# First convolution of a four-layer block: nine taps in five groups of 128 rows, with a second set of copies

## The chip, the cores and the metric

The kernel runs on one core of a Trainium2 chip. The metric is the device time of one execution in microseconds; several executions are run and their median is given. A core has five engines that run their own instruction streams and meet only at semaphores: TensorE (PE in the profile; PEld are its weight loads), VectorE (DVE), ScalarE (ACT), GpSimd (POOL) and SyncE (SP, which here only issues DMAs). Sixteen DMA engines move data.

## The reference

Input x is 32 images of 64 channels, 28 x 28 pixels, in float32. Four layers follow one another, each of the form `x = x + layer(group_norm(x))`. The change touches only the first, a convolution whose 3 x 3 weights are mixed per image from four candidates:

```
pooled = mean(x, axis=(2, 3));  h = relu(pooled @ fc1_w.T)
prob = softmax((h @ fc2_w.T + fc2_b).reshape(B, 4, 64) / 4, axis=1)
agg_w = einsum('bko,koihw->boihw', prob, weight)     # 64 x 64 x 3 x 3 per image
out = conv(x, agg_w), 3 x 3, stride 1, padding 1, one set of weights per image
```

Layer 1 is a quantised convolution, layer 2 a two-dimensional cosine transform, layer 3 self-attention over the 784 pixels with four heads.

## The kernel before, in words

All 32 images stay on the chip as 16 pairs: an image has 64 channels, so a pair fills the 128 partitions (image 0 of the pair in partitions 0 to 63, image 1 in 64 to 127). Layers run one after another over all pairs. Every engine has its own program for a layer (`l0` for the first), written with four pairs unrolled, a loop over the middle ones, and two unrolled at the end; `pair_steps` and `looped` do that. The order on each engine is the order of the text.

The first convolution, pair p, goes through these steps:

- **mix** (DVE, lines 1265 to 1277): four operations of 128 x 576 on the candidates `w0` give the pair's weights `agg[p % 2]`, output channels in partitions, taps and input channels along the row.
- **pad** (DVE, line 1285): each image is normalised into its own padded tile of 30 x 30, `pads[p % 2][im]`, image 0 in partitions 0 to 63 and image 1 in 64 to 127. After the second of them `s_pad` rises.
- **twin** (SP, lines 416 and 417): two DMAs fill the other 64 partitions of the two tiles with the same image shifted by one pixel. So 128 partitions hold two horizontally neighbouring taps, and one matmul over 128 rows does both.
- **transposes** (PE, lines 832 to 840): `agg` is turned so that input channels lie in partitions, in six transposes: three of two taps (128 rows out) and three of the single third tap of an image row (64 rows out). ACT (lines 652 and 653) copies them to `pair_w` and `last_w`.
- **convolution** (PE, line 861): for each half c of the image (14 image rows, 392 columns) twelve matmuls accumulate into one bank: three of 128 rows (the first two taps of each row of the 3 x 3 window) and three of 64 rows (the third tap), each for both images of the pair. The two images' matmuls use different halves of the array's columns. The transposes of pair p + 1 stand between the two halves of pair p.
- **add, statistics** (DVE, lines 1300 and 1170 to 1173): each half is added to x when it is done, and after the second half the statistics for the next layer are taken; then comes pad of pair p + 2.

Before the first matmul of a pair PE waits for the copied weights (line 845) and for the twins (line 846):

```
pe.wait_ge(s_convw, lin(lambda q: q + 1, p, i, 2))
pe.wait_ge(s_twin[p % 2], lin(lambda q: 32 * (q // 2 + 1), p, i, 2))
```

Tiles are doubled by p % 2, and pad of pair p + 2 waits for the end of pair p's convolution, since it writes the tile that pair p reads. All float32 matmuls appear as two records each in the profile (two passes).

Of the kernel before, what the change touches and what calls it, by code (L numbers as in the profile page):

```python
# [14 lines left out]
B, C, H, W = 32, 64, 28, 28  # L15
T = H * W
NP = B // 2
HC = H // 2
CH = HC * W
BANK = 512  # L20
HID, KEXP = 16, 4
NG, GC = 4, 16
HP, WP = H + 2, W + 2
# [16 lines left out]
ACT = mybir.ActivationFunctionType  # L40
# [14 lines left out]
    _at += _width  # L55
PARAMS = _at
W0_COLS = KEXP * C * 9
W1_ROWS = GC * 3 * 2
W1_COLS = NG * 3 * 128

# [5 lines left out]
def build(nc, x_in, params, w0_in, w1_in, out):  # L66
    ctx = ExitStack()
    with ctx:
# [6 lines left out]
        x = sb("x", [128, NP, T])  # L75
        par = sb("par", [128, PARAMS])

        def P(name, rows=128):
            return par[0:rows, AT[name][0]:AT[name][1]]
# [24 lines left out]
        def part(shape, dt=F32):  # L104
            n = int(np.prod(shape[1:])) * mybir.dt.size(dt) // 4
            a = arena[0:shape[0], cut[0]:cut[0] + n]
            cut[0] += n
            assert cut[0] <= ARENA, cut[0]
            if dt is not F32:
                a = a.bitcast(dt)  # L110
            names = " ".join("abcde"[:len(shape) - 1])
            if len(shape) > 2:
                a = a.rearrange(f"p ({names}) -> p {names}", **dict(zip("abcde", shape[1:])))
            return a


        w0 = part([128, KEXP, 9 * C])
        agg = [part([128, 9, C]) for _ in range(2)]
        pair_w = [part([128, 3, 128]) for _ in range(2)]
        last_w = [part([C, 3, 128]) for _ in range(2)]  # L120


        PAD = HP * WP + 4
        pads = [[part([128, PAD]) for _ in range(2)] for _ in range(2)]
        pooled = part([128, NP])
        hid = part([2 * HID, NP])
        logit = part([128, NP, KEXP])
# [52 lines left out]
        ps = ctx.enter_context(nc.psum_tensor("ps", [128, 8, BANK], F32))  # L180
# [16 lines left out]
        def lin(f, s0, i, per):  # L197

            return f(s0) if i is None else i * (f(s0 + per) - f(s0)) + f(s0)
# [17 lines left out]
        s_convw = sem("s_convw")  # L217
        s_pad = sem("s_pad")
        s_twin = [sem(f"s_twin{n}") for n in range(2)]
# [177 lines left out]
        def _(sp):  # L397
# [14 lines left out]
            def twin_step(p, i):  # L412

                first, second = pads[p % 2]
                wait_apart(sp, s_pad, lin(lambda q: q + 1, p, i, 2))
                sp.dma_start(first[C:2 * C, 0:HP * WP - 1], first[0:C, 1:HP * WP]).then_inc(s_twin[p % 2], 16)
                sp.dma_start(second[0:C, 1:HP * WP + 1], second[C:2 * C, 0:HP * WP]).then_inc(s_twin[p % 2], 16)

            pair_steps(twin_step, sp)

# [216 lines left out]
        def _(act):  # L637
# [9 lines left out]
            def l0(p, i):  # L647

                act.wait_ge(s_aggt, lin(lambda q: q + 1, p, i, 2))
                if p >= 2:  # L650
                    act.wait_ge(s_conv, lin(lambda q: 2 * (q - 1), p, i, 2))
                nc.scalar.activation(pair_w[p % 2].rearrange("p y n -> p (y n)"), ps[:, 0, 0:3 * 128], ACT.Copy)  # L652
                nc.scalar.activation(last_w[p % 2].rearrange("p y n -> p (y n)"), ps[0:C, 1, 0:3 * 128],
                                     ACT.Copy).then_inc(s_convw, 1)

            pair_steps(l0, act)

# [144 lines left out]
            n = at_ring(B - 1, NU - 1) + 1  # L802
# [4 lines left out]
        def _(pe):  # L807
# [16 lines left out]
            for k in range(KEXP):  # L824
                last = nc.tensor.matmul(ps[:, 5, k * NP:(k + 1) * NP],
                                        P("fc2", 2 * HID)[:, k * 128:(k + 1) * 128],
                                        hid[:, :], start=True, stop=True)
            last.then_inc(s_l0t, 1)

            def l0_transpose(p, i):  # L830

                pe.wait_ge(s_agg, lin(lambda q: q + 1, p, i, 2))
                if p >= 1:
                    pe.wait_ge(s_convw, lin(lambda q: q, p, i, 2))
                for y in range(3):
                    n = slice(y * 128, (y + 1) * 128)
                    nc.tensor.transpose(ps[:, 0, n],
                                        agg[p % 2][:, 3 * y:3 * y + 2, :].rearrange("p t i -> p (t i)"), P("ident"))
                    last = nc.tensor.transpose(ps[0:C, 1, n], agg[p % 2][:, 3 * y + 2, :], P("ident"))  # L839
                last.then_inc(s_aggt, 1)  # L840

            def l0(p, i):
                if p == 0:
                    l0_transpose(0, None)
                pe.wait_ge(s_convw, lin(lambda q: q + 1, p, i, 2))
                pe.wait_ge(s_twin[p % 2], lin(lambda q: 32 * (q // 2 + 1), p, i, 2))
                for c in range(2):
                    bank = 3 + 2 * (p % 2) + c
                    if p >= 2:
                        pe.wait_ge(s_added, lin(lambda q: 2 * (q - 2) + c + 1, p, i, 2))  # L850


                    for single in range(2):
                        for y in range(3):
                            for im in range(2):
                                rows = slice(0, C if single else 128)
                                w = (last_w if single else pair_w)[p % 2][:, y, im * C:(im + 1) * C]
                                at = (y + c * HC) * WP + 2 * single + im
                                rhs = pads[p % 2][im][rows, at:at + HC * WP].rearrange(
                                    "p (y x) -> p y x", x=WP)[:, :, 0:W]  # L860
                                last = nc.tensor.matmul(ps[im * C:(im + 1) * C, bank, 0:CH], w, rhs,  # L861
                                                        start=(y == 0 and not single), stop=(y == 2 and single == 1))
                    last.then_inc(s_conv, 1)
                    if c == 0 and p + 1 < NP:
                        l0_transpose(p + 1, i)
# [278 lines left out]
            n = at_ring(B - 1, NU - 1) + 1  # L1144
# [7 lines left out]
        def _(dve):  # L1152
# [54 lines left out]
                chain[0], chain[2] = start + links * rounds, None  # L1207


            for pair in pads:  # L1210
                for b in pair:
                    last = v.memset(b[:, :], 0.0)
# [49 lines left out]
            def mix(p, i):  # L1262

                pr = at_pair(p, i)
                a = agg[p % 2].rearrange("p t i -> p (t i)")

                def weight(k):
                    return prob[:, bass.ds(pr, 1), k]

                if p >= 2:  # L1270
                    dve.wait_ge(s_aggt, lin(lambda q: q - 1, p, i, 2))
                link(v.tensor_scalar(a, w0[:, 0, :], weight(0), None, ALU.mult))
                for k in range(1, KEXP):
                    last = v.scalar_tensor_tensor(a, w0[:, k, :], weight(k), a, ALU.mult, ALU.add)
                    if k < KEXP - 1:
                        link(last)
                last.then_inc(s_agg, 1)
# [233 lines left out]
def pack(a):  # L1511
# [16 lines left out]
    n = W  # L1528
# [28 lines left out]
    put("head_rows", np.kron(np.eye(NH, dtype=f), np.ones((1, 2 * DK), f)), slice(0, NH))  # L1557


    w0 = a["L0_conv_weight"].transpose(1, 0, 3, 4, 2).reshape(C, W0_COLS)  # L1560
    w0 = np.ascontiguousarray(np.tile(w0, (2, 1)))

    w1 = a["L1_conv_weight"].reshape(C, NG, GC, 3, 3).transpose(2, 4, 1, 3, 0)
# [18 lines left out]
```

## Time and profile before

| | us |
|---|---|
| median of 3 runs | 1832.68 |
| lowest, highest | 1827.34, 1839.15 |
| the profiled execution's own time | 1829.92 |
| its span | 1828.1 |
| mean granted clock of PE | 0.949 |

| engine | busy us | share of the span |
|---|---|---|
| PE | 1663.0 | 91% |
| DVE | 1285.1 | 70% |
| ACT | 1022.2 | 56% |
| POOL | 434.1 | 24% |

The first convolution lies between 62.3 and 212.9 us of the span. Times in the rows are counted from the span's start. A row of the timeline gives start, duration, engine, line, operation, output and input tile and number of instructions, merged where they follow one another; in brackets stands the idle time before and what ended it. SPq is the queue of DMA issues: such a row is the issuing, not the transfer. "PEclk" is the granted clock as a share of full speed: 1.00 is 2.4 GHz, 0.50 is 1.2 GHz.

### The profile page before, as it was taken

How to read it: one execution, taken by the hardware profiler on the slowest of the kernel's cores; microseconds unless marked ns; L12 is line 12 of the kernel's file. 1: busy time of each engine (PE TensorE's matmuls, PEld its weight loads, DVE VectorE, ACT ScalarE, POOL GpSimd, SP SyncE). 2: the span in 40 equal slices, each digit the busy share in tenths (PEclk: the TensorE clock that was granted, in tenths of full speed). 3: DMA queues.
4: the chain of work that ended last, by engine and by line, in shares of the span. 5: the costliest groups of instructions: out<-in, count | busy, mean ns of one | idle time of the engine just before them, and what ended most of it. 6: DMA issues, size and time to landing. Idle time of an engine off the chain costs nothing.

```text
span 1828.1 us, 35089 instructions
## 1 busy us (share of the span) xinstructions
PE 1663.0 (91%) x10910; PEld 751.8 (41%) x10910; DVE 1285.1 (70%) x2603; ACT 1022.2 (56%) x1401; POOL 434.1 (24%) x333
## 2 busy tenths in 40 slices
PE   0799689997884999999999999999999999999997
PEld 0333245554873244444434434434443443444332
DVE  5677467887784887777767767666776776767762
ACT  0100166674331176777767667666676776767676
POOL 0400011112102212423413223232341423323111
PEclk9999899999897599999999989989999999999999
DMA  8111166663002332332233322332322332224300
GB/s 197 41 51 45 40 108 100 109 102 54 0 0 33 50 43 33 48 58 43 35 48 50 49 43 33 47 51 46 48 33 43 53 53 43 33 47 54 47 11 19
DMA packets 70267, 93.31 MB, mean 51 GB/s; under 512 B 22648, under 2 KB 63224, under 8 KB 69968
## 3 DMA queue, kind: packets, MB, share of 16 engines
q1 hardware_dynamic: 67728, 89.59, 29.9%
q0 software_dynamic: 2368, 1.57, 1.0%
q8 instruction: 92, 1.51, 0.3%
q14 instruction: 79, 0.65, 0.1%
HBM read 9.00 MB, written 6.42 MB: 8 GB/s over the span
## 4 chain that ended last, share of the span: by engine, by line
PE 81%; DVE 6%; ACT 4%; DMA 3%; SPq 3%; issue 3%; DVEq 0%; POOL 0%; ACTq 0%; POOLq 0%
PE ps L1051 20%; PE ps L1041 18%; PE ps L986 16%; PE ps L861 8%; PE ps L885 5%; PE ps L900 3%; PE ps L1032 3%; PE ps L1007 2%; ACT arena L679 2%; DMA x<-x_in 2%; PE ps L947 2%; SPq L433 2%; PE ps L1024 1%; DVE arena L1430 1%; PE ps L1015 1%
## 5 line engine op out<-in xcount | busy, mean ns | idle before, releaser
L1430 DVE TENSOR_REDUCE arena<-ps 128x1 f32<-128x392 f32 x1600 | 827.0, 559 | 329.5 <-PE ps L986 316.1
L792 ACT ACTIVATE arena<-ps 112x784 f32<-112x784 f32 x896 | 703.4, 822 | 270.4 <-PE ps L1041 265.8
L986 PE MATMUL ps<-arena 112*128 112x392 bf16 x1536 | 491.1, 348 | 8.7 <-DMA arena<-arena 8.2
L1041 PE MATMUL ps<-arena 114*112 114x392 bf16 x1792 | 457.1, 342 | 19.9 <-issue 14.8
L1051 PE MATMUL ps<-arena 112*32 112x392 f32 x3584 | 401.2, 520 | 0.4 <-ACT arena L792 0.4
L986 PEld LDWEIGHTS ps<-arena 112*128 112x128 bf16 x1536 | 151.2, 99 | 377.4 <-DVE arena L1430 307.5
L1041 PEld LDWEIGHTS ps<-arena 114*112 114x112 bf16 x1792 | 230.2, 136 | 140.7 <-issue 50.8
L885 PE MATMUL ps<-arena 96*128 96x392 f16 x768 | 142.2, 336 | 22.0 <-DMA arena<-arena 16.5
L679 ACT ACTIVATE arena<-ps,magic,arena 128x784 f32<-128x784 f32 x128 | 128.2, 1004 | 37.2 <-PE ps L885 37.0
L861 PE MATMUL ps<-arena 128*64 128x392 f32 (+1 forms) x768 | 139.5, 505 | 3.9 <-DMA arena<-arena 3.9
L1051 PEld LDWEIGHTS ps<-arena 112*32 112x32 f32 x3584 | 71.3, 109 | 147.7 <-issue 146.0
L885 PEld LDWEIGHTS ps<-arena 96*128 96x128 f16 x768 | 67.5, 98 | 95.3 <-ACT arena L679 29.4
L529 POOL TENSOR_TENSOR arena<-arena 128x784 f16<-128x784 f32 x16 | 26.0, 1626 | 324.9 <-ACT arena L668 324.9
L1337 DVE TENSOR_SCALAR arena<-arena 128x784 bf16<-128x784 f32 x128 | 73.1, 571 | 32.3 <-ACT arena L679 21.6
L600 POOL TENSOR_TENSOR arena<-arena 128x784 f32<-128x784 f32 x31 | 57.4, 1852 | 122.3 <-ACT arena L749 122.3
L861 PEld LDWEIGHTS ps<-arena 128*64 128x64 f32 (+1 forms) x768 | 49.6, 135 | 86.4 <-issue 84.2
L652 ACT ACTIVATE arena<-ps 128x384 f32<-128x384 f32 x16 | 7.9, 492 | 134.3 <-PE ps L839 134.3
L595 POOL DMA_DIRECT2D arena<-arena x31 | 21.3, 687 | 251.8 <-DVE arena L1445 234.6
L694 ACT ACTIVATE arena<-ps 112x512 f32<-112x512 f32 x64 | 31.0, 542 | 67.9 <-PE ps L944 67.8
L569 POOL TENSOR_TENSOR x<-x,arena 128x784 f32 (+1 forms) x16 | 29.6, 1853 | 161.4 <-DVE arena L1423 161.4
L900 PE MATMUL ps<-arena 128*64 128x392 bf16 x768 | 66.5, 329 | 0.0
L628 POOL TENSOR_TENSOR x<-x,arena 128x784 f32 (+1 forms) x15 | 27.9, 1863 | 160.0 <-ACT arena L743 160.0
(139 smaller groups left out, 1381.9 us busy)
## 6 DMA issues: line engine op xcount, KB each, us to landing
arena<-arena SPq DMA_DIRECT2D x504, 73.5 KB, 2.7
arena<-arena SPq DMA_DIRECT2D x256, 84.2 KB, 2.8
x<-x_in SPq DMA_DIRECT2D x8, 784.0 KB, 21.2
out<-x SPq DMA_DIRECT2D x16, 392.0 KB, 2.4
arena<-arena SPq DMA_DIRECT2D x252, 24.5 KB, 2.3
arena<-arena SPq DMA_DIRECT2D x256, 1.5 KB
arena<-arena SPq DMA_DIRECT2D x16, 225.0 KB, 3.4
arena<-arena SPq DMA_DIRECT2D x16, 224.8 KB, 2.9
```

The source lines that it names most:

```text
L600: nc.gpsimd.tensor_tensor(a, a, den[:, :], ALU.mult).then_inc(s_head, 1)
L679: nc.scalar.activation(halves(rounded[u % 4]), two(2 * (u % 2)), ACT.Identity, bias=magic[:, 0:1], scale=ratio[:, u % NG:u % NG + 1]).then ...
L792: nc.scalar.activation(probs[w % 2][:, 2 * pair:2 * pair + 2, :], two(2 * place, rows=slice(0, TT)), ACT.Exp).then_inc(s_taken, 1)
L861: last = nc.tensor.matmul(ps[im * C:(im + 1) * C, bank, 0:CH], w, rhs, start=(y == 0 and not single), stop=(y == 2 and single == 1))
L885: last = nc.tensor.matmul(ps[:, 2 * (u % 2) + c, 0:CH], w1[:, g, y, :], rhs, start=(y == 0), stop=(y == 2))
L900: last = nc.tensor.matmul(ps[im * C:(im + 1) * C, bank + c, 0:CH], sdiag[:, k, g, :], quant[2 * (p % 2) + im][:, g, c * CH:(c + 1) * CH], ...
L986: last = nc.tensor.matmul(ps[:, bank, 0:CH], q[0:ROWS_L, h, it * 128:(it + 1) * 128], k[0:ROWS_L, h, c * CH:(c + 1) * CH], start=True, sto ...
L1032: last = nc.tensor.matmul(ps[:, 2 * place + c, 0:CH], P("head_rows", NH), den_row[:, c * CH:(c + 1) * CH], start=True, stop=True)
L1041: last = nc.tensor.matmul(ps[0:TT, 2 * place + j, 0:CH], ks[s % 4][0:ROWS_ALL, h, jt * TT:(jt + 1) * TT], qs[s % 4][0:ROWS_ALL, h, c * CH: ...
L1051: last = nc.tensor.matmul(ps[32 * h:32 * h + 32, BANK_ACC, 0:CH], vs[s % 4][:, jt, h, :], probs[w % 2][:, h, :], start=(jt == 0), stop=(jt ...
L1337: link(v.tensor_scalar(capped[:, :], rounded[u % 4][:, :], MAGIC, QP, ALU.subtract, ALU.min))
L1430: nc.vector.tensor_reduce(mx[img % 2][:, c, v:v + 1], scores, AX.X, ALU.max).then_inc(s_mf, 1)
```

## The change

The nine taps are stored in another order, `TAPS`: the first two of each row of the window, then the three third taps, and a tenth place in `agg` that is set to zero once. Five groups of two taps (`UNITS`) replace three groups of two and three of one. Groups 0 to 2 are as before. Group 3 holds the third taps of the window's rows 0 and 1; it reads new tiles, `rows_pads`, whose partitions 0 to 63 hold the image and 64 to 127 the image shifted up by one row (30 elements). Group 4 holds the third tap of row 2 beside the zero weights and reads `pads`. Four DMAs more per pair fill the two new tiles, two for each image; PE now waits for six DMAs of a pair (96) in place of two (32). There are five transposes of 128 x 128 in place of six, and the two ACT copies take 512 and 128 columns of all partitions.

```diff
+TAPS = [(y, x) for y in range(3) for x in range(2)] + [(0, 2), (1, 2), (2, 2)]
+UNITS = 5
-        agg = [part([128, 9, C]) for _ in range(2)]
-        pair_w = [part([128, 3, 128]) for _ in range(2)]
-        last_w = [part([C, 3, 128]) for _ in range(2)]
+        agg = [part([128, 2 * UNITS, C]) for _ in range(2)]
+        pair_w = [part([128, UNITS, 128]) for _ in range(2)]
+        rows_pads = [[part([128, HP * WP]) for _ in range(2)] for _ in range(2)]
...
                 sp.dma_start(second[0:C, 1:HP * WP + 1], second[C:2 * C, 0:HP * WP]).then_inc(s_twin[p % 2], 16)
+                for to, data in zip(rows_pads[p % 2], (first[0:C], second[C:2 * C])):
+                    sp.dma_start(to[0:C, :], data[:, 0:HP * WP]).then_inc(s_twin[p % 2], 16)
+                    sp.dma_start(to[C:2 * C, 0:(HP - 1) * WP], data[:, WP:HP * WP]).then_inc(s_twin[p % 2], 16)
...
-                for y in range(3):
-                    n = slice(y * 128, (y + 1) * 128)
-                    nc.tensor.transpose(ps[:, 0, n],
-                                        agg[p % 2][:, 3 * y:3 * y + 2, :].rearrange("p t i -> p (t i)"), P("ident"))
-                    last = nc.tensor.transpose(ps[0:C, 1, n], agg[p % 2][:, 3 * y + 2, :], P("ident"))
+                for n in range(UNITS):
+                    last = nc.tensor.transpose(ps[:, n // 4, (n % 4) * 128:(n % 4 + 1) * 128],
+                                               agg[p % 2][:, 2 * n:2 * n + 2, :].rearrange("p t i -> p (t i)"),
+                                               P("ident"))
...
-                pe.wait_ge(s_twin[p % 2], lin(lambda q: 32 * (q // 2 + 1), p, i, 2))
+                pe.wait_ge(s_twin[p % 2], lin(lambda q: 96 * (q // 2 + 1), p, i, 2))
...
-                    for single in range(2):
-                        for y in range(3):
-                            for im in range(2):
-                                rows = slice(0, C if single else 128)
-                                w = (last_w if single else pair_w)[p % 2][:, y, im * C:(im + 1) * C]
-                                at = (y + c * HC) * WP + 2 * single + im
-                                rhs = pads[p % 2][im][rows, at:at + HC * WP].rearrange(
-                                    "p (y x) -> p y x", x=WP)[:, :, 0:W]
-                                last = nc.tensor.matmul(ps[im * C:(im + 1) * C, bank, 0:CH], w, rhs,
-                                                        start=(y == 0 and not single), stop=(y == 2 and single == 1))
+                    for n in range(UNITS):
+                        y, x_ = TAPS[2 * n]
+                        for im in range(2):
+                            by_rows = n == 3
+                            src = (rows_pads if by_rows else pads)[p % 2][im]
+                            at = (y + c * HC) * WP + x_ + (0 if by_rows else im)
+                            rhs = src[:, at:at + HC * WP].rearrange("p (y x) -> p y x", x=WP)[:, :, 0:W]
+                            last = nc.tensor.matmul(ps[im * C:(im + 1) * C, bank, 0:CH],
+                                                    pair_w[p % 2][:, n, im * C:(im + 1) * C], rhs,
+                                                    start=(n == 0), stop=(n == UNITS - 1))
...
+            for a in agg:
+                v.memset(a[:, 9, :], 0.0)
...
-    w0 = a["L0_conv_weight"].transpose(1, 0, 3, 4, 2).reshape(C, W0_COLS)
+    w0 = a["L0_conv_weight"].transpose(1, 0, 3, 4, 2)
+    w0 = np.stack([w0[:, :, y, x] for y, x in TAPS], 2).reshape(C, W0_COLS)
```

On SP, the copies of pairs 0 and 1 in the kernel before, each pair behind its own wait for `s_pad`:

```order
L416 DMA arena<-arena 64x899
L417 DMA arena<-arena 64x900
L416 DMA arena<-arena 64x899
L417 DMA arena<-arena 64x900
```

The same place in the changed kernel, pair 0 alone (then the same six for pair 1):

```order
L420 DMA arena<-arena 64x899
L421 DMA arena<-arena 64x900
L423 DMA arena<-arena 64x900
L424 DMA arena<-arena 64x870
L423 DMA arena<-arena 64x900
L424 DMA arena<-arena 64x870
```

The old two copies go first; the four new ones stand behind them in the same queue, and PE's wait is for all six.

On PE, the transposes of pair 0 and the first half of its convolution, before:

```order
L837 MATMUL ps<-par,arena 128x128
L839 MATMUL ps<-par,arena 64x128
L837 MATMUL ps<-par,arena 128x128
L839 MATMUL ps<-par,arena 64x128
L837 MATMUL ps<-par,arena 128x128
L839 MATMUL ps<-par,arena 64x128
L861 MATMUL ps<-arena 64x392 x12
```

and now, with the transposes of pair 1 and what follows them:

```order
L842 MATMUL ps<-par,arena 128x128 x5
L865 MATMUL ps<-arena 64x392 x10
L842 MATMUL ps<-par,arena 128x128 x5
L865 MATMUL ps<-arena 64x392 x20
```

Ten matmuls stand in place of twelve in each half, and nothing else has moved on PE.

## Rows read from the trace of the kernel before

**Rows 1.** The page: the chain that ended last, share of the span by line.

```profile
PE ps L1051 20%; PE ps L1041 18%; PE ps L986 16%; PE ps L861 8%; PE ps L885 5%; PE ps L900 3%; PE ps L1032 3%; PE ps L1007 2%; ACT arena L679 2%; DMA x<-x_in 2%; PE ps L947 2%; SPq L433 2%; PE ps L1024 1%; DVE arena L1430 1%; PE ps L1015 1%
```

**Rows 2.** The chain in order of time, first convolution (start us, us, what).

```profile
58.28 0.55 SPq L416
58.87 3.37 DMA arena<-arena
...
62.37 6.54 PE ps L861 x24
...
78.22 0.26 PE ps L837
...
79.03 8.51 PE ps L861 x48
...
212.96 0.57 DVE x L1300
```

**Rows 3.** Timeline of PEld, one pair: the weight loads stand where passes begin.

```profile
73.90 0.20 PEld L861 LDWEIGHTS ps<-arena 128*64 128x64 f32 x4 [0.61 <-issue]
...
76.03 0.20 PEld L861 LDWEIGHTS ps<-arena 64*64 64x64 f32 x4 [0.61 <-issue]
...
78.15 0.14 PEld L837 LDWEIGHTS ps<-par,arena 128*128 128x128 f32 x1 [0.61 <-issue]
...
78.96 0.20 PEld L861 LDWEIGHTS ps<-arena 128*64 128x64 f32 x4 [0.20 <-issue]
...
83.22 0.20 PEld L861 LDWEIGHTS ps<-arena 128*64 128x64 f32 x4 [0.61 <-issue]
```

**Rows 4.** Timeline of DVE after the last matmul of pair 0.

```profile
74.02 0.56 DVE L1300 TENSOR_TENSOR x<-x,ps 128x392 f32<-128x392 f32 x1 [1.50 <-PE ps L861]
...
76.13 1.39 DVE L1285 TENSOR_SCALAR arena<-x,gmean,grstd 64x784 f32<-64x784 f32 x2
78.27 0.56 DVE L1300 TENSOR_TENSOR x<-x,ps 128x392 f32<-128x392 f32 x1 [0.75 <-PE ps L861]
...
79.30 2.53 DVE L1274 SCALAR_TENSOR_TENSOR arena<-arena 128x576 f32<-128x576 f32 x3
```

**Rows 5.** Timeline of SP: the issue of pair 2's two copies.

```profile
77.55 0.46 SPq L416 DMA_DIRECT2D arena<-arena  x1
78.06 0.60 SPq L417 DMA_DIRECT2D arena<-arena  x1
```

**Rows 6.** Line 417, the second copy: time from issue to landing.

```profile
DMA to landing us min/median/max: 3.3/3.4/4.0
```

**Rows 7.** Windows (window, us, busy of PE, PEld, DVE, ACT, POOL, PEclk, DMA share, GB/s).

```profile
78.67:79.82 1.15, 1.15 (x10) 0.57 (x10) 1.11 (x3) 0.75 (x2) 0.00 (x0) 1.00 0.99 203
79.82:80.67 0.85, 0.85 (x9) 0.29 (x4) 0.81 (x2) 0.11 (x1) 0.00 (x0) 1.00 0.73 267
```

**Rows 8.** Timeline of PEld at the first pair's start.

```profile
63.71 0.26 PEld L861 LDWEIGHTS ps<-arena 128*64 128x64 f32 x2 [0.39 <-issue]
64.36 0.26 PEld L861 LDWEIGHTS ps<-arena 128*64 128x64 f32 x2 [0.39 <-issue]
...
67.43 0.14 PEld L861 LDWEIGHTS ps<-arena 64*64 64x64 f32 x2 [0.19 <-issue]
67.76 0.14 PEld L861 LDWEIGHTS ps<-arena 64*64 64x64 f32 x2 [0.19 <-issue]
```

**Rows 9.** Windows around two idle stretches of PE in later layers.

```profile
240.65:243.44 2.79, 0.00 (x1) 0.01 (x1) 2.51 (x5) 1.04 (x2) 0.00 (x0) 1.00 0.81 132
243.44:247.88 4.44, 4.44 (x17) 2.17 (x18) 1.41 (x4) 2.87 (x3) 1.63 (x1) 0.62 0.81 132
...
577.27:581.17 3.90, 0.00 (x1) 0.01 (x1) 3.74 (x6) 1.10 (x4) 0.35 (x1) 1.00 0.00 0
581.17:582.40 1.23, 1.23 (x4) 0.81 (x5) 0.00 (x0) 0.00 (x0) 1.22 (x3) 1.00 0.38 51
582.40:585.59 3.19, 3.19 (x6) 1.07 (x4) 0.00 (x0) 0.91 (x1) 3.19 (x8) 0.50 0.93 114
```

More of the change, by code:

```diff
@@ L651, in l0 @@
                     act.wait_ge(s_conv, lin(lambda q: 2 * (q - 1), p, i, 2))
-                nc.scalar.activation(pair_w[p % 2].rearrange("p y n -> p (y n)"), ps[:, 0, 0:3 * 128], ACT.Copy)
-                nc.scalar.activation(last_w[p % 2].rearrange("p y n -> p (y n)"), ps[0:C, 1, 0:3 * 128],
-                                     ACT.Copy).then_inc(s_convw, 1)
+                nc.scalar.activation(pair_w[p % 2][:, 0:4, :].rearrange("p y n -> p (y n)"), ps[:, 0, 0:BANK], ACT.Copy)
+                nc.scalar.activation(pair_w[p % 2][:, 4, :], ps[:, 1, 0:128], ACT.Copy).then_inc(s_convw, 1)
             pair_steps(l0, act)
@@ L1264, in mix @@
                 pr = at_pair(p, i)
-                a = agg[p % 2].rearrange("p t i -> p (t i)")
+                a = agg[p % 2][:, 0:9, :].rearrange("p t i -> p (t i)")
                 def weight(k):
```

## The prediction

> **What bounds the kernel now.** I read the page's chain first: the first convolution is 8% of it by its matmul line [rows 1], so the change can only reach that stage. The chain in order of time shows the stage's shape [rows 2]: one wait for the first pair's copies, and from 62.37 us to 212.96 nothing but matmuls and transposes, one round of 8.51 us plus transposes per pair. PE is the bound. The weight loads give the round exactly [rows 3]: pair 1 starts at 73.90 and pair 2 at 83.22, which is 9.32 us. Sixteen pairs of it make the stage.
>
> What stands next in line is not seen in the chain, and the change works on it: the time from the end of one pair's matmuls to the arrival of the copies that the pair after next needs. The rows of DVE, SP and DMA give it. Pair 0 ends at 73.90; DVE adds the second half at 74.02, takes statistics and writes the padded tiles of pair 2 until 77.52 (76.13 + 1.39) [rows 4]; SP issues the two copies at 77.55 and 78.06 [rows 5]; data moves from 78.67 to 80.67 [rows 7]; the second copy lands 3.4 us after its issue [rows 6], at 81.46. Pair 2 starts at 83.22. **The slack is 1.76 us**, and every pair has it.
>
> **PE's part of the change.** Half a pair is six passes at 128 rows (73.90 to 76.03) and six at 64 rows (76.03 to 78.15), 2.13 us each [rows 3]. Between neighbouring passes lie 0.33 us (67.43 to 67.76 [rows 8]), six of them 1.96, so each block has 0.17 us more, where the row count of the weights changes. The transposes take 78.15 to 78.96, 0.81 us. A pair is 4 x 2.13 + 0.81 = 9.33. After the change a half has ten passes, all of 128 rows: 3.27 us. The change of shape remains only before the transposes (0.17), and a transpose less at 0.11 us each leaves 0.70. A pair is 2 x 3.27 + 0.17 + 0.70 = **7.4 us of PE**, 1.9 less. Were PE still the bound, the stage would lose 15 x 1.9, about 29 us, 1.6% of the kernel.
>
> DVE could follow: after the second half it works 3.50 us (74.02 to 77.52) and after the first one 3.56 (78.27 to 81.83) [rows 4], 7.1 in all, within 7.4. The larger ACT copy sits after the transposes with 3.3 us of matmuls to hide it. The two memsets of 64 columns on DVE lie in the wait for x at the start. All of these I cost at nothing; without PE's cover DVE would set 7.1.
>
> **The copies.** Six take the place of two, all of the same size within 4%, in one queue; PE waits for the last. The two now take 1.15 and 0.85 us of data time, and in that time the DMA engines are 0.99 and 0.73 busy at 203 and 267 GB/s [rows 7]. So they are limited by moving bytes, not by issue: SP issues one in 0.5 to 0.65 us and stays ahead. Of the four new ones, two go to partitions 0 to 63 and two to 64 to 127, as one and one do now. Two more such sets cost 2 x 2.0 = 4.0 us end to end, or 2 x (0.99 x 1.15 + 0.73 x 0.85) = 3.5 if the engines never pause between them. I take **3.7**. The landing moves from 81.46 to 85.16, that is from 7.56 to 11.26 us after the pair's end; with the step to the first matmul (landing at 62.24, matmul at 62.37 [rows 2]) 11.4.
>
> The slack is gone: pair 1 begins as pair 0 ends and needs 7.4, so PE then stands idle for 11.4 - 7.4 = **4.0 us**, works off pair 2 and, its copies having come meanwhile, pair 3, and idles again. The loop is over two pairs: 11.4 + 7.4 = 18.8, and 0.05 to 0.1 for the drain, against 2 x 9.32 = 18.64 now. Seven such loops (ends of pairs 0 to 14) give +1.5 us. The first pair starts 3.7 later and ends its own work 1.9 earlier, +1.8; the last pair saves 1.8 behind the last loop. Sum without the clock: **+1.5 us**. The whole gain of PE is eaten by the later landing.
>
> **The clock.** Now PE never rests in this stage. At its start it ran at the lower of its levels: passes of a pair of images 0.65 us apart (63.71 to 64.36) and, once warm, 0.33 (67.43 to 67.76) [rows 8]; until the change at 66.98 that cost about 2.3 us (half of 62.37 to 66.98). Two idle stretches of other layers show what a rest of such length does [rows 9]: PE idle for 2.79 us, and in the 4.44 behind it the granted clock is 0.62 (most of it at 1.2 GHz); idle for 3.90 us, then 1.23 us at 1.00 and the next 3.19 at 0.50. So each gap of 4.0 should cost half of 3.4 us at least, 1.7, and up to the 2.3 of the start. I take 2.0, seven times: **+14 us**. It enters the loop fully, since the slowed pair's end starts the next copies. The Trainium skill (TensorE: Matmul & The Clock Gate, "HAM oscillation — how this bites in real kernels") describes this for a loop that waits on a DMA in each round: it restarts at the lower clock every round. By that rule all seven gaps pay; the two stretches agree.
>
> **Sum.** 1.5 + 14, about +15 us on the profiled execution's 1829.92 us: 1845. The median of the runs stands 2.8 above that execution, so 1847 for the median. The other layers keep their instructions; only addresses move.
>
> **The rivals.**
> (a) *As forecast*, copies bound the loop and the clock falls in each gap. With 3.5 to 4.0 for the copies and 1.7 to 2.3 for the clock: (-1.4 to +2.1) + (12 to 16) + 1.5, +12 to +20. For it: the DMA engines' shares and both idle stretches. Chance 0.60.
> (b) *The clock holds.* The other layers' matmuls have other shapes, and two stretches are few. +1.5: 1834. Chance 0.09.
> (c) *Faster: the four new copies move at the rate of the second copy's best, so the gap shrinks.* At 0.85 and less each, since its engines are only 0.73 busy (0.62 of busy time): 4 x 0.62 = 2.5 in place of 3.7, seven loops of -1.2, -8; gap 2.8, where a fall is not certain: 0 to +12. Between 1826 and 1838. It would be a gain above 1% from a loop of 16.0 us on (18.64 less 18.3 / 7), a landing less than 1 us later than now; PE alone would be the bound only if the copies landed no later than now, and the time 1804. Against it: 900 KB would have to move in 1 us, four times the rate of the row. Chance 0.11, of which 0.04 above 1%. The Trainium skill (DMA: Bandwidth & Descriptors, "Anatomy of one DMA — SWDGE (gpsimd) path") fits a transfer as 2.0 us plus bytes over 436 GB/s; by it the four new copies would add 2.1 us, not 3.7, and the time would be about that of this rival. The trace does not bear it out: 203 and 267 GB/s.
> (d) *Slower: all four new copies move like the first, not like the second.* The first differs from the second in its target (partitions 64 to 127) and its source address (off by one element); which counts no row tells. At 1.15 each the landing is 4.6 later, at more queueing 5.5: seven loops of +0.9 to +1.8 on top, gap 4.9 to 5.8 with the same fall or a longer one. +22 to +32: 1854 to 1864. It decides from a landing 4.2 us later. Chance 0.20.
>
> **How the numbers follow.** What this kernel's measurement can tell from no change is about 1%, 18 us. Slower by more: (d) and the upper fifth of (a), 0.20 + 0.13 = 0.33. Faster by more: 0.04. Within: 0.63. The range takes in (a) and (b), the slower half of (c) and nearly all of (d), with some 3 us for the spread of a median: 1829 to 1863. (a) alone spans 1845 to 1852.
>
> **What the new profile would show.** PEld's timeline: a pair of 7.4 us and no shape change inside a half. SP: six issues per pair in some 3.7 us. Windows: DMA share near 0.9 for 5.5 to 6 us per pair. PE: an idle stretch of about 4 us ended by the copies before every other pair (2, 4, ..., 14), and none before the odd ones. PEclk: 0.50 for 3 to 5 us behind each. Stage end near 228 us in place of 212.96. The forecast is wrong if copies of SBUF data overlap better than the two of today show, if gaps come before every pair (another loop than mine), or if later layers shift.

## The result, and the profile after

| | before | after |
|---|---|---|
| median us (runs) | 1833.28 (4) | 1858.37 (4) |
| lowest to highest | 1827.34 to 1839.15 | 1849.85 to 1861.05 |
| profiled execution, its span | 1829.92, 1828.1 | 1861.05, 1859.2 |
| mean granted clock | 0.949 | 0.933 |
| first convolution, first to last matmul | 62.37 to 212.92 | 67.00 to 237.58 |

The ratio is 1.0129, with a 95% interval of 1.0082 to 1.0176. The change makes the kernel **slower by 25 us**. The first convolution alone ends 24.7 us later (237.58 against 212.92), which is about the whole difference of the medians (25.1); the profiled execution of after is the slowest of its four, with 5 us more in the attention layer.

PE's part did what it was meant to. This is PE's timeline of the changed kernel: two rows on the form of a pair, then the rows before which PE was idle (in brackets: for how long and what ended it).

```profile
73.85 6.81 PE L865 MATMUL ps<-arena 128*64 128x392 f32 x40
...
81.29 3.51 PE L865 MATMUL ps<-arena 128*64 128x392 f32 x20
88.97 5.21 PE L865 MATMUL ps<-arena 128*64 128x392 f32 x20 [4.17 <-issue]
...
110.06 5.18 PE L865 MATMUL ps<-arena 128*64 128x392 f32 x20 [4.30 <-DMA arena<-arena]
...
132.09 6.11 PE L865 MATMUL ps<-arena 128*64 128x392 f32 x20 [5.27 <-DMA arena<-arena]
...
154.81 5.00 PE L865 MATMUL ps<-arena 128*64 128x392 f32 x20 [5.02 <-DMA arena<-arena]
...
176.42 6.13 PE L865 MATMUL ps<-arena 128*64 128x392 f32 x20 [5.04 <-DMA arena<-arena]
...
199.17 5.01 PE L865 MATMUL ps<-arena 128*64 128x392 f32 x20 [5.04 <-DMA arena<-arena]
...
220.66 6.19 PE L865 MATMUL ps<-arena 128*64 128x392 f32 x20 [4.91 <-issue]
```

The second halves of pairs 0 and 1 start at 73.85 and 81.29: a pair takes 7.44 us in place of 9.32 [rows 3]. But PE is idle for 4.2 to 5.3 us before pairs 2, 4, ..., 14, where before it was never idle ([rows 2]: 8.51 us of matmuls, transposes, 8.51 us). Each first half behind a gap takes 5.0 to 6.2 us; the same ten matmuls at full clock take 3.5. Windows over the stage, before and then after (window, us, busy of PE, PEld, DVE, ACT, POOL, PEclk, DMA share, GB/s), and over two of the slow halves:

```profile
62.37:212.92 150.55, 150.55 (x858) 58.64 (x858) 99.06 (x177) 14.18 (x31) 3.71 (x4) 1.00 0.18 46
```

```profile
67.00:237.58 170.58, 136.83 (x715) 58.12 (x715) 97.91 (x175) 12.79 (x31) 0.00 (x0) 0.90 0.52 119
88.97:94.17 5.20, 5.20 (x21) 2.29 (x22) 0.00 (x0) 0.00 (x0) 0.00 (x0) 0.67 0.93 219
132.09:138.20 6.11, 6.11 (x21) 2.21 (x22) 0.00 (x0) 0.00 (x0) 0.00 (x0) 0.57 0.89 206
```

PE's busy time fell only from 150.55 to 136.83 us although a sixth of the matmuls went, since 0.10 of the clock is missing: at half clock that is 34 us of the 170.58 (the start of the stage, slow before and after, is not recorded in PEclk). The seven slow halves (38.8 us together, against 7 x 3.52) cost **14.2 us**. The idle time costs 33.8 us (170.58 less 136.83) and the later start 4.6; PE's shorter pairs take 28 us off.

The chain through one loop, pair 4's second half to pair 6's first (start, us, what):

```profile
115.94 3.47 PE ps L865 x20
...
119.89 0.57 DVE x L1307
...
124.00 0.47 SPq L420
...
127.14 4.83 DMA arena<-arena
...
132.09 6.11 PE ps L865 x20
```

Where the chain before was PE alone, it now runs PE, DVE, SP, DMA, PE. From the second add at 119.89 to the next matmul are 12.20 us: DVE 4.11 until the issue at 124.00, and 8.09 from issue to matmul, where before 4.04 lay between (77.55 to 81.46 and the 0.13 of the step) [rows 5, 6]. So four copies more make the landing **4.05 us** later. Windows over the copies of pair 2, whose first is issued at 80.94, and the time to landing of line 424, the last of each tile:

```profile
83.00:84.00 1.00, 1.00 (x10) 0.44 (x8) 0.96 (x2) 0.00 (x0) 0.00 (x0) 1.00 0.96 295
...
86.00:87.00 1.00, 0.00 (x0) 0.00 (x0) 0.90 (x5) 0.00 (x0) 0.00 (x0) 1.00 1.04 229
87.00:88.10 1.10, 0.00 (x0) 0.00 (x0) 1.08 (x2) 0.00 (x0) 0.00 (x0) 1.00 0.73 161
```

```profile
DMA to landing us min/median/max: 4.3/4.8/6.0
```

The DMA engines are full until about 87 us, against shares of 0.99 and 0.73 with two copies [rows 7]. The new copies' first packets start 0.96 to 1.00 us apart in the trace: about 1.0 us each, whichever half of the partitions they go to and whether their source is shifted or not. The old two keep their form in the longer queue: the third copy starts 0.63 us behind the second.

### The profile page after: what moved, and what is told of

Its sections match the earlier page's. It is cut to its first block, busy times and chain, and to the rows that moved or that the text cites. A ratio compares the mean times of both kernels' runs of the same rounds, so it can differ in the third digit from the quotient of the medians.

```text
span 1859.2 us, 34867 instructions
## 1 busy us (share of the span) xinstructions
PE 1657.9 (89%) x10766; PEld 754.1 (41%) x10766; DVE 1285.3 (69%) x2605; ACT 1021.8 (55%) x1401; POOL 434.1 (23%) x333
## 4 chain that ended last, share of the span: by engine, by line
PE 77%; DVE 7%; DMA 5%; SPq 4%; issue 4%; ACT 3%; DVEq 0%; POOL 0%; ACTq 0%; POOLq 0%
PE ps L1056 19%; PE ps L1046 17%; PE ps L991 16%; PE ps L865 6%; PE ps L890 4%; DMA arena<-arena 3%; PE ps L905 3%; PE ps L1037 3%; PE ps L1012 2%; SPq L440 2%; DMA x<-x_in 2%; ACT arena L685 2%; PE ps L952 2%; PE ps L1029 1%; DVE arena L1437 1%
## 5 line engine op out<-in xcount | busy, mean ns | idle before, releaser
L865 PE MATMUL ps<-arena 128*64 128x392 f32 x640 | 127.4, 555 | 42.1 <-DMA arena<-arena 33.0
L659 ACT ACTIVATE arena<-ps 128x512 f32<-128x512 f32 x16 | 9.6, 599 | 162.7 <-PE ps L842 162.7
L1344 DVE TENSOR_SCALAR arena<-arena 128x784 bf16<-128x784 f32 x128 | 73.1, 571 | 32.3 <-ACT arena L685 21.5
L865 PEld LDWEIGHTS ps<-arena 128*64 128x64 f32 x640 | 50.2, 153 | 111.3 <-issue 110.9
```

What stands on the lines that cost most here:

```text
L1344: link(v.tensor_scalar(capped[:, :], rounded[u % 4][:, :], MAGIC, QP, ALU.subtract, ALU.min))
```

## The experiments

The theory after the result: the loop of two pairs is set by the path from a pair's end over DVE, SP and the six copies to the pair after next, and the clock falls in the gaps that this opens. Its rivals: the new form of the matmuls is slow itself; the slow halves come from PE reading beside the DMAs; one DMA queue, not the engines, is the limit. Each window row that begins at the stage's start covers the first convolution from its first to its last matmul; the stage before took 150.55 us and after 170.58. Ratios are to the kernel before, run beside each experiment.

**Copies alone** (`e1_copies_only`, on the kernel before):

```diff
+        rows_pads = [[part([128, HP * WP]) for _ in range(2)] for _ in range(2)]
...
+                for to, data in zip(rows_pads[p % 2], (first[0:C], second[C:2 * C])):
+                    sp.dma_start(to[0:C, :], data[:, 0:HP * WP]).then_inc(s_twin[p % 2], 16)
+                    sp.dma_start(to[C:2 * C, 0:(HP - 1) * WP], data[:, WP:HP * WP]).then_inc(s_twin[p % 2], 16)
...
-                pe.wait_ge(s_twin[p % 2], lin(lambda q: 32 * (q // 2 + 1), p, i, 2))
+                pe.wait_ge(s_twin[p % 2], lin(lambda q: 96 * (q // 2 + 1), p, i, 2))
```

> The kernel before with the four new copies per pair, waited for, and with its own twelve matmuls per half; nothing reads the new tiles. Theory (the landing of the copies sets the loop): the copies land 4.0 us later, so about 12.2 us lie between a pair's end and the start of the pair after next inside the loop, and with 9.3 us of PE a loop of two pairs takes 21.5 in place of 18.64. Seven loops and the later start: PE idle 2.3 to 2.9 us before every other pair, first layer ends 20 to 24 us later if the clock holds in such gaps, up to 32 if it falls in each; 1853 to 1865 us. Rival (the copies run beside PE at no cost, the loss comes from the new matmuls): only the first pair starts 4 us later, 1833 to 1839 us.

Median 1873.10 (5 runs), ratio 1.0221 (1.0182 to 1.0260). Its windows over the stage and over one first half, and PE's first two idle stretches:

```profile
66.84:259.74 192.90, 171.80 (x858) 64.87 (x858) 98.35 (x175) 14.18 (x31) 0.00 (x0) 0.87 0.46 105
115.63:123.86 8.23, 8.23 (x24) 2.47 (x24) 1.12 (x2) 0.00 (x0) 0.00 (x0) 0.50 0.72 166
```

```profile
89.60 7.12 PE L865 MATMUL ps<-arena 128*64 128x392 f32 x24 [2.33 <-issue]
...
115.63 8.30 PE L865 MATMUL ps<-arena 128*64 128x392 f32 x24 [2.42 <-DMA arena<-arena]
```

The gaps are 2.3 to 3.8 us, five of the seven above the 2.3 to 2.9 of the theory, and the rival's 1839 is out. The waits come near the theory: the six loops from pair 2 to pair 14 took 24.97 us each, of which 3.1 are PE's work taking longer than at full clock, and 21.8 stand against the 21.5 expected.

The median is 8 us above the theory's highest. In the trace the stage ends 46.8 us later than before, and 21 of them are PE's work at the lower clock: 50 us of the stage at 1.2 GHz, against 34 us and a cost of 14 in the changed kernel. Behind the gap at 115.63 the whole first half ran at 0.50. But this is the slowest of the five executions, 1882.08 where the others took 1870.93 to 1873.28. Less those 9 us the clock costs about 12, and the median's 40.4 over the kernel before leave 15 (both estimates from these numbers). So the theory allowed too little for the clock, 8 us; that shorter gaps cost more than long ones is not shown.

**PE's form alone** (`e2_two_copies`, on the changed kernel):

```diff
-                for to, data in zip(rows_pads[p % 2], (first[0:C], second[C:2 * C])):
-                    sp.dma_start(to[0:C, :], data[:, 0:HP * WP]).then_inc(s_twin[p % 2], 16)
-                    sp.dma_start(to[C:2 * C, 0:(HP - 1) * WP], data[:, WP:HP * WP]).then_inc(s_twin[p % 2], 16)
...
-                pe.wait_ge(s_twin[p % 2], lin(lambda q: 96 * (q // 2 + 1), p, i, 2))
+                pe.wait_ge(s_twin[p % 2], lin(lambda q: 32 * (q // 2 + 1), p, i, 2))
...
-                            by_rows = n == 3
+                            by_rows = False
```

> The changed kernel without its four new copies: group 3 reads the old tiles, so two taps of the window are computed from the wrong pixels; PE's work is that of the changed kernel. Theory: the landing goes back to about 8.1 us behind a pair's end, against 7.4 us of PE, so the loop takes 15.5 to 15.9 us, PE idles under 1 us before every other pair, the clock never falls in the layer, and the layer is 22 to 25 us shorter than before the change: 1808 to 1812 us. DVE, with 7.7 us per pair in its loop, is then as near to the bound. Rival (the five-group form itself is slow on PE): no faster than 1830.

Median 1813.76 (4 runs), ratio 0.9889 (0.9844 to 0.9934).

```profile
62.37:189.95 127.58, 123.37 (x715) 53.72 (x715) 98.63 (x177) 12.77 (x31) 3.70 (x4) 1.00 0.21 55
```

```profile
111.26 3.52 PE L862 MATMUL ps<-arena 128*64 128x392 f32 x20 [1.04 <-DMA arena<-arena]
...
119.19 3.52 PE L862 MATMUL ps<-arena 128*64 128x392 f32 x20 [0.26 <-DMA arena<-arena]
```

The stage is 23 us shorter than before at a clock of 1.00, with 0.3 to 0.5 us of idle time per pair in the loop after one of 1.04. The median is 2 us above the range expected. The five groups are no slower than priced; 45 us lie between this kernel and the changed one, and all of them come with the four copies.

**The clock by itself** (`e3_filled_gap`, on the changed kernel):

```diff
+                if p % 2 == 0 and p >= 2:
+                    for _ in range(6):
+                        nc.tensor.matmul(ps[:, 2, 0:CH], P("ident"), par[:, 0:CH], start=True, stop=True)
                 pe.wait_ge(s_twin[p % 2], lin(lambda q: 96 * (q // 2 + 1), p, i, 2))
```

> The changed kernel with six float32 matmuls of 128 x 392 on constant data into a free bank before the wait of every even pair from the third on (about 3.9 us of work into a gap of 4.2 to 5.3 us). Theory (the waits and the clock are two costs): the gaps stay, but the granted clock stays at 1.00 through the layer; the first halves behind a gap take 3.5 us in place of 5.0 to 6.2, seven times 2.07 less, so 14 us less than the changed kernel: about 1844 us, 10 above the kernel before. Rival (the slow first halves come from PE reading tiles that DMAs are writing beside): they stay at 5.0 to 6.2 us and the time at 1858.

Median 1848.48 (6 runs), ratio 1.0085 (1.0052 to 1.0118).

```profile
67.12:224.05 156.93, 151.54 (x799) 68.30 (x799) 97.89 (x175) 12.77 (x31) 0.00 (x0) 1.00 0.56 129
```

```profile
122.98 4.22 PE L853 MATMUL ps<-par 128*128 128x392 f32 x12
128.32 3.51 PE L868 MATMUL ps<-arena 128*64 128x392 f32 x20 [1.12 <-DMA arena<-arena]
```

With 4.2 us of idle work ahead of the same wait, the clock is 1.00 through the stage, the halves behind the wait take 3.5 us with the same DMAs running, and the stage is 156.93 us, 13.7 less than after. So the slow halves come from the clock and not from reading beside DMAs. Against the changed kernel the medians differ by 10 us where 14 were expected, and the ranges leave 14 open; the stage is the sharper measure.

**A later wait** (`e4_rows_last`, on the changed kernel):

```diff
-                    sp.dma_start(to[0:C, :], data[:, 0:HP * WP]).then_inc(s_twin[p % 2], 16)
-                    sp.dma_start(to[C:2 * C, 0:(HP - 1) * WP], data[:, WP:HP * WP]).then_inc(s_twin[p % 2], 16)
+                    sp.dma_start(to[0:C, :], data[:, 0:HP * WP]).then_inc(s_rows[p % 2], 16)
+                    sp.dma_start(to[C:2 * C, 0:(HP - 1) * WP], data[:, WP:HP * WP]).then_inc(s_rows[p % 2], 16)
...
-                pe.wait_ge(s_twin[p % 2], lin(lambda q: 96 * (q // 2 + 1), p, i, 2))
+                pe.wait_ge(s_twin[p % 2], lin(lambda q: 32 * (q // 2 + 1), p, i, 2))
...
-                    for n in range(UNITS):
+                    for n in (0, 1, 2, 4, 3):
+                        if n == 3 and c == 0:
+                            pe.wait_ge(s_rows[p % 2], lin(lambda q: 64 * (q // 2 + 1), p, i, 2))
...
```

> The changed kernel with a semaphore of its own for the four new copies and group 3 put last in each half, so that PE starts a pair when the two old copies have landed and waits for the new ones only after four groups. Theory: PE starts about 8.1 us behind a pair's end, has 2.6 us of work and then waits some 1.4 us more for the new copies; loop 8.1 + 1.4 + 7.4 = 16.9 to 17.2 us, no fall of the clock: 10 to 14 us faster than before the change, 1819 to 1823 us. Rival (the DMA queue itself is full, so that the old copies of a pair wait behind the new ones of the pair before): the old copies land later too, loop near 19, 1833 or more.

Median 1823.12 (10 runs), ratio 0.9936 (0.9909 to 0.9963): faster than before by 0.6%.

```profile
62.43:199.12 136.69, 124.67 (x715) 51.98 (x715) 98.53 (x176) 12.78 (x31) 3.56 (x4) 1.00 0.68 155
```

```profile
131.14 2.86 PE L868 MATMUL ps<-arena 128*64 128x392 f32 x16 [0.80 <-DMA arena<-arena]
134.98 0.88 PE L868 MATMUL ps<-arena 128*64 128x392 f32 x4 [0.98 <-DMA arena<-arena]
```

Two short waits, 0.80 and 0.98 us, stand where one of 5 stood (1.4 us were expected for the second), and the clock holds. The same bytes move in the same queue; only what waits for them has changed.

**DVE's loop** (`e8_unrolled`, on the changed kernel):

```diff
-            for p in range(4):
-                l0(p, None)
-            looped(l0, PAIR_LOOP, 2 * 6)
-            for p in (NP - 2, NP - 1):
-                l0(p, None)
+            for p in range(NP):
                 l0(p, None)
```

> The changed kernel with DVE's program for the first layer written out for all 16 pairs in place of a loop over ten of them. In the trace of the changed kernel DVE takes 4.0 us from the second add to the end of the padded tiles inside the loop and 3.5 outside (each link between two of its instructions costs 0.15 us more), and it comes to the second add 0.46 us late. Theory (these 0.9 us stand in the path from a pair's end to the landing): five loops of 0.9 us, 4 to 5 us off the changed kernel, PE's gaps inside the loop 4.1 to 4.3 us as outside in place of 5.0: 1852 to 1855 us. Rival (the longer gaps come from the DMA queue): gaps and time unchanged.

Median 1854.09 (4 runs), ratio 1.0122 (1.0076 to 1.0167).

```profile
66.39:231.84 165.45, 135.42 (x715) 57.80 (x715) 98.33 (x175) 12.77 (x31) 0.00 (x0) 0.91 0.53 123
```

```profile
130.66 5.20 PE L865 MATMUL ps<-arena 128*64 128x392 f32 x20 [4.34 <-DMA arena<-arena]
```

The gaps inside the loop are 4.3 us in place of 5.0, and the stage is 5.1 us shorter. Only 3.7 of them are shorter gaps (all seven 30.0 us together, against 33.8). Another 1.3 are the very first half, which took 4.94 us in place of 6.22. Its ten matmuls took anything between in e2, e3, e9, e10 and e11 too, and no edit touches them.

**Two queues** (`e9_second_queue` and `e10_second_queue_early`): ScalarE issues the four new copies on its own queue, in e9 behind its copies of the weights and in e10 ahead of its wait for the transposes. SyncE's lines for them go. The edit of e10:

```diff
             def l0(p, i):
...
+                first, second = pads[p % 2]
+                act.wait_ge(s_pad, lin(lambda q: q + 1, p, i, 2))
+                for to, data in zip(rows_pads[p % 2], (first[0:C], second[C:2 * C])):
+                    nc.scalar.dma_start(to[0:C, :], data[:, 0:HP * WP]).then_inc(s_twin[p % 2], 16)
+                    nc.scalar.dma_start(to[C:2 * C, 0:(HP - 1) * WP], data[:, WP:HP * WP]).then_inc(s_twin[p % 2], 16)
                 act.wait_ge(s_aggt, lin(lambda q: q + 1, p, i, 2))
```

> The changed kernel with the four new copies issued by ScalarE on its own DMA queue, beside the two old ones on SyncE's. Theory (the sixteen DMA engines are full: 0.9 busy at some 220 GB/s): the last copy of a pair lands about 7.5 to 8 us behind the issue of the first, as now, PE's gaps stay at 4 to 5 us, 1855 to 1860 us; if anything the issues overlap and save 0.5 us per loop. Rival (one queue handles its DMAs one behind the other): the six land after 4.5 to 5 us, the gaps shrink to 1 to 2 us, 1820 to 1830 us.

e9: median 1866.90 (4 runs), ratio 1.0197 (1.0147 to 1.0247). PE's timeline:

```profile
111.75 4.85 PE L867 MATMUL ps<-arena 128*64 128x392 f32 x20 [2.88 <-DMA arena<-arena]
...
123.77 5.21 PE L867 MATMUL ps<-arena 128*64 128x392 f32 x20 [3.03 <-DMA arena<-arena]
```

Both expectations missed, since the kernel made a wait of its own: ScalarE reaches the issues only after the transposes of the pair before, so PE waits 2.7 to 3.0 us before *every* pair. It says nothing on queues, and so e10 was made.

> As e9_second_queue, but ScalarE issues the four new copies ahead of its wait for the transposes, so that both queues start as soon as the padded tiles are written. Theory (the DMA engines, not the queue, are the limit: a copy of 225 KB costs 1.0 us on whichever queue): PE's gaps are again 4 to 5 us before every other pair only, 1855 to 1860 us. Rival (each queue handles its DMAs one behind the other): landing after 5 to 6 us, gaps of 2 to 3 us, 1835 to 1845 us.

e10: median 1858.24 (10 runs), ratio 1.0116 (1.0086 to 1.0147). The stage, and two pieces of the chain, from the first issue on ScalarE's queue to pair 6's first matmul:

```profile
66.52:236.58 170.06, 135.24 (x715) 57.45 (x715) 97.89 (x175) 12.77 (x31) 0.00 (x0) 0.90 0.51 119
```

```profile
123.83 0.49 ACTq L656
...
132.14 4.96 PE ps L867 x20
```

From issue to matmul are 8.31 us, against 8.09 on one queue; the gaps are 4.2 to 5.4. Two queues move the six copies no faster, and the rival is out. The limit is not the queue; the DMA engines are the busy part (shares of 0.96 to 1.05 above), and whether it is they or the memory that they read and write, no run parts.

**Two copies fewer** (`e11_act_bases`, on the changed kernel): ScalarE writes the unshifted half of each new tile; for the second image the other half is shifted down by a row in place of up.

```diff
+                act.wait_ge(s_pad, lin(lambda q: q + 1, p, i, 2))
+                for im in range(2):
+                    r = slice(im * C, (im + 1) * C)
+                    nc.scalar.activation(rows_pads[p % 2][im][r, 0:HP * WP], pads[p % 2][im][r, 0:HP * WP], ACT.Copy)
...
+                up, down = rows_pads[p % 2]
+                sp.dma_start(up[C:2 * C, 0:(HP - 1) * WP], first[0:C, WP:HP * WP]).then_inc(s_twin[p % 2], 16)
+                sp.dma_start(down[0:C, WP:(HP + 1) * WP], second[C:2 * C, 0:HP * WP]).then_inc(s_twin[p % 2], 16)
...
-                            at = (y + c * HC) * WP + x_ + (0 if by_rows else im)
+                            at = (y + c * HC) * WP + x_ + im * (WP if by_rows else 1)
```

> The changed kernel with the two unshifted copies written by ScalarE from the padded tiles (64 x 900 each), so that four DMAs per pair are left in place of six. Theory (each copy in the queue costs the landing 1.0 us): it comes 2.0 us earlier than in the changed kernel, PE's gaps before every other pair are 2.2 to 3.0 us in place of 4.2 to 5.0, and the clock falls in some of them: 14 us less for the gaps and 0 to 14 us less for the clock, 1830 to 1844 us. Rival (the landing hangs on the last copy's own latency and not on how many stand before it): no change to the changed kernel, 1858.

Median 1831.66 (10 runs), ratio 0.9989 (0.9956 to 1.0021): no change to before.

```profile
64.06:209.90 145.84, 127.10 (x715) 55.24 (x715) 97.92 (x175) 40.20 (x60) 1.81 (x3) 0.96 0.38 94
```

```profile
100.00 5.21 PE L869 MATMUL ps<-arena 128*64 128x392 f32 x20 [2.21 <-DMA arena<-arena]
...
119.91 3.52 PE L869 MATMUL ps<-arena 128*64 128x392 f32 x20 [3.13 <-DMA arena<-arena]
...
137.92 5.21 PE L869 MATMUL ps<-arena 128*64 128x392 f32 x20 [2.37 <-DMA arena<-arena]
```

The gaps are 2.1 to 3.1 us, two less than after, as a price of 1.0 us per copy says, and the clock fell in three of seven. The time lies in the range expected.

**The version that the runs point to** (`e5_rows_after_both`, on e4): PE takes groups 0, 1, 2 and 4 of both halves first and group 3 of both last; DVE mixes the next weights ahead of its adds.

```diff
+                groups(0, (0, 1, 2, 4))
+                if p + 1 < NP:
+                    l0_transpose(p + 1, i)
+                groups(1, (0, 1, 2, 4))
+                pe.wait_ge(s_rows[p % 2], lin(lambda q: 64 * (q // 2 + 1), p, i, 2))
+                for c in range(2):
+                    groups(c, (3,)).then_inc(s_conv, 1)
...
             def l0(p, i):
+                if p + 2 < NP:
+                    mix(p + 2, i)
                 for c in range(2):
-                    if c == 0 and p + 2 < NP:
-                        mix(p + 2, i)
```

> As e4_rows_last, but group 3 of both halves stands behind the other four groups of both, and DVE mixes the weights of pair p + 2 before it adds pair p in place of between its halves. Theory: 6 us of PE's work now lie in front of the wait for the new copies, which land 4 us behind the old ones, so that wait vanishes; what is left are PE's 7.4 us, DVE's 7.7 in its loop and 8.1 + 7.4 for the loop of two pairs: 7.8 us per pair, as with two copies only. 22 to 25 us less than before the change: 1808 to 1812 us. Rival (the copies of the next pair then queue behind the new ones of this one and the wait moves there): 8.5 us per pair, 1820.

Median 1815.73 (7 runs), ratio 0.9915 (0.9889 to 0.9941).

```profile
62.45:190.85 128.40, 123.01 (x715) 53.36 (x715) 99.63 (x176) 12.77 (x31) 3.56 (x4) 1.00 0.72 165
```

```profile
127.81 2.85 PE L864 MATMUL ps<-arena 128*64 128x392 f32 x16 [0.64 <-DMA arena<-arena]
...
135.72 2.86 PE L864 MATMUL ps<-arena 128*64 128x392 f32 x16 [0.26 <-DVE x L1314]
```

All six copies are there and the stage is 22 us shorter than before, within 1 us of the kernel without them (127.58). The wait for the new copies is gone. The theory's 7.8 us per pair and 1812 us were missed, and so were the rival's 8.5 and 1820. What is left is the wait for the old copies, 0.64 us before pair 8, and a short one for DVE, 0.26 us before pair 9: a pair takes 8.08 us (127.81 to 143.97 for two).

**With DVE written out** (`e6_after_both_unrolled`: e5 with the edit of e8).

> e5_rows_after_both with DVE's first layer written out as in e8_unrolled. Theory: DVE needs 7.1 us per pair, the way from a pair's end to the start of the pair after next is 7.6 us, so the loop of two pairs is 15.0 us: 4 us less than e5, 1804 to 1808 us. Rival (PE's 7.4 us and not DVE hold e5): no difference to e5 beyond 1 us in the trace.

Median 1812.19 (5 runs), ratio 0.9895 (0.9851 to 0.9939), the fastest that ran.

```profile
62.51:187.22 124.71, 122.97 (x715) 53.41 (x715) 100.56 (x176) 12.78 (x31) 3.55 (x4) 1.00 0.74 170
```

```profile
114.31 7.01 PE L864 MATMUL ps<-arena 128*64 128x392 f32 x40
...
129.75 7.09 PE L864 MATMUL ps<-arena 128*64 128x392 f32 x40
```

PE is idle for 0.2 us here and there; a pair takes 7.7 us (two in 15.44). The stage is 3.7 us shorter than e5's, so that DVE's loop did hold e5 and the rival is out. But the medians of e5 and e6 are not apart beyond their spread: 4 us less were expected, and the median lies 4 us above the range. The traced execution, 1802.33, is the fastest of the five.

## Why the prediction was right, and where a term was too small

The forecast was 1847 us in a range of 1829 to 1863, with 0.63 on no change beyond 1% and 0.33 on slower; measured were 1858, 1.3% slower. The mechanism was right: copies bound a loop over two pairs, PE gains its 1.9 us per pair and waits them off, gaps before the even pairs only, a fall of the clock in each. The size was too small, by 11 us of 25, so that a slowdown beyond 1% came where no change was called likelier. The time lies outside (a)'s 1845 to 1852 and inside (d)'s 1854 to 1864, but the landing moved by 4.05 us and not by the 4.2 from which (d) counts. The range reached that far only for (d)'s sake, while most of the excess came from DVE and from the start: that it held the time is in part luck.

- **PE's part**: 7.4 us per pair forecast, 7.44 measured. e2 shows that alone it would have been worth 23 us of the stage, near the 29 that PE as the only bound would give; DVE and the two old copies take the rest.
- **The copies**: 3.7 us later forecast, 4.05 measured. Seven loops of 0.35: 2.4 us. Rival (d) asked whether target or source address makes the first copy slow. Neither does by itself: the four new ones go to both halves of the partitions, with and without a shifted source, and take 1.0 us each. Their packets took 260 to 279 ns at the median, as the first copy's 278; the second copy's took 141, before and after. So the 0.85 us of the second copy [rows 7] was no price for the new ones. What makes it faster is open.
- **DVE**: the term that was sized wrongest. "All of these I cost at nothing" held for its throughput only because PE waited: in the loop DVE needs 7.8 us per pair (4.0 behind the second add, 3.8 behind the first), more than PE's 7.4 and than the 7.1 that I had read. And DVE's 3.5 us from second add to padded tiles stood in my path, and I read them at pair 0 [rows 4], which is written out. Inside the loop, where waits are computed from a counter, the kernel before already shows 4.0 (120.71 to 124.70), with idle time before instructions that wait for the one ahead. So "every pair has it" was wrong of the slack too: the copies are issued at 124.80 and pair 7 starts at 129.80, 5.00 us of which 4.04 are needed, and 0.96 are left in place of 1.76.

```profile
120.71 0.56 DVE L1300 TENSOR_TENSOR x<-x,ps 128x392 f32 x1 [1.04 <-PE ps L861]
...
123.31 1.39 DVE L1285 TENSOR_SCALAR arena<-x,gmean,grstd 64x784 f32 x2 [0.18 <-DVE mv L1173]
...
124.80 0.46 SPq L416 DMA_DIRECT2D arena<-arena  x1
...
129.80 0.20 PEld L861 LDWEIGHTS ps<-arena 128*64 128x64 f32 x4 [0.61 <-issue]
```

In the changed kernel the second add is late as well. In pair 4 it starts at 119.89, 4.02 us behind the start of PE's half (115.87), outside the loop 3.56. The mix ahead of it ends at 119.34, before PE's half does, and DVE then stands idle for 0.55 us:

```profile
117.56 1.78 DVE L1281 SCALAR_TENSOR_TENSOR arena<-arena 128x576 f32<-128x576 f32 x2 [0.15 <-DVE arena L1281]
119.89 0.56 DVE L1307 TENSOR_TENSOR x<-x,ps 128x392 f32 x1 [0.55 <-PE ps L865]
...
122.50 1.39 DVE L1292 TENSOR_SCALAR arena<-x,gmean,grstd 64x784 f32 x2 [0.19 <-DVE mv L1178]
```

In pairs 6, 8, 10 and 12 the add is 0.23 us late. With the 0.5 of the path behind it that is 3.8 us in five loops. e8, without DVE's loop, took 3.7 us off the gaps; which part of the loop costs the time, no run shows. Before the change the slack covered it.
- **The clock**: +14 us forecast, 14.2 in the slow halves, 13.7 by e3.
- **The start**: the first matmul came 4.6 us later in place of 3.7 (0.4 of it before the first issue), and the first pair, with its first half at half clock, saved 1.2 in place of 1.9: 1.6 us.

15.5 + 2.4 + 3.8 + 1.6 + 0.2 is 23.5 of the 24.7 us of the stage; 1.2 us stay unassigned. Rival (b), the clock holds, fell, and so did rival (c), faster by quicker copies: four copies of 225 KB took 4.05 us more, about 220 GB/s. The Trainium skill's fit of bytes over 436 GB/s (DMA: Bandwidth & Descriptors, "Anatomy of one DMA — SWDGE (gpsimd) path") is stated there for transfers issued by GpSimd; these are issued by SyncE, and it did not hold for them.

## What to carry to other kernels

Before work is moved from the bounding engine to copies, add up the path from the moment that a buffer is free to the moment that its copies land, over all engines on it, and compare it with the work that hides it: here about 1 us of slack in the loop met 4.05 us of copies, and a saving of 1.9 us per pair became a loss. Read such a path in the rows of the loop, not of the unrolled start. And let work that needs few copies go first: the same six copies cost 25 us when all are waited for at the start of a pair, and the kernel came out 10 us faster than before when the group that needs them stood last in each half (e4), and 16 us faster when it stood behind both halves and DVE's mix ahead of its adds (e5).

## What the runs showed of the hardware beyond this

- A gap's length alone did not tell whether the clock fell. In e11 it fell in gaps of 2.21, 2.37 and 2.41 us and held in gaps of 2.09, 2.82, 2.93 and 3.13. In the changed kernel, e8 and e10 it fell in all 21 of 4.2 to 5.4.
- What a gap costs is not fixed by its length either. In the traced execution of e1 gaps of 2.3 to 3.8 us cost 21 us of PE's time, in the changed kernel gaps of 4.2 to 5.3 cost 14; but that execution of e1 was 9 us slower than the other four.
- Copies between partitions of one core's SBUF ran at about 1.0 us per 225 KB with the DMA engines' shares at 0.96 to 1.05 (the four new ones, one behind the other on one queue), and two queues moved the six no faster. One copy of the six, the second, was quicker, with packets of 141 ns against 260 to 279.
